# Four pairs ahead of the repeating step, rounded halves for the feed-forward's first products, and another order of the step

## The chip, the cores and the metric

The kernel runs on one core of one Trainium2 chip. The metric is device time in microseconds (us), the median of several runs; smaller is better. TensorE does the matrix products and transposes, VectorE and ScalarE read its results from PSUM (eight banks of 128 x 512 float32), GpSimd works on SBUF alone, and the DMA queues load and store.

## The reference

Sixteen batches of 128 tokens x 128 features pass a gated cross-attention over a context of 120 x 96, then two layers of windowed attention with a gated feed-forward, and a gated residual at the end. Cut to what matters here:

```python
def _layer(x, wqkv, qs, ksc, wo, lg, lb, w1, b1, w2, b2):
    h = shift_token(x)
    q, k, v = jnp.split(h @ wqkv, 3, axis=-1)     # 8 heads of 64
    q, k = rotary_xpos(l2norm(q) * qs, l2norm(k) * ksc)
    x = x + local_attention(q, k, v) @ wo
    h = shift_token(x)
    h = (h - mu) / jnp.sqrt(var + 1e-05) * lg + lb
    a, g = jnp.split(h @ w1 + b1, 2, axis=-1)     # 341 + 341 columns
    return x + (a * jax.nn.gelu(g, approximate=False)) @ w2 + b2
```

All inputs and the output are float32.

## The kernel before

**Work.** The cross-attention runs on pairs of batches (eight pairs). The layers run on 32 batch-layer items i (16 batches, then the same for layer 1). The feed-forward runs on groups of four items: seven full groups 0 to 6, and the last four items as two groups of two, 7 and 8. The residual stream is held transposed in `xs`, features on partitions.

**Step.** Every engine runs the same loop over a step number n and calls, in a written order, the functions whose item, pair or group is due: `project_k(n+5)`, `project_q(n+4)`, `squares` and `turns` (rotary products), `rows_q/rows_k(n+2)` (transposes), `scores_(n+2)`, `maxima_(n+1)` on VectorE, `weights(n+1)` (the exponentials, with `pp` and its sums) on ScalarE, `normalise(n+1)` on GpSimd, `weights_T(n+1)` (transposes of the probabilities), `weights_out` (their copy `pT` to SBUF, on ScalarE), `attend(n+1)`, `out_proj(n)`. On TensorE a step begins with `rows_k` and ends with scores, `weights_T`, `project_k` and `attend`. Each engine executes in its written order, so one waiting instruction holds all behind it. Lines such as `if s.n == -17` place single calls that have no fixed place in the loop: those of the first pairs and of the last two groups.

**Group in the step.** For group g, step 4g+4 holds `deviation`, `variance`, `dev_rstd` and `normed_h` (the normalised `hn`); step 4g+5, here called the gate step, holds three products `gate_in_0/1/2` of 128, 128 and 85 rows x 512 columns; step 4g+6, the value step, holds `value_in_0/1/2` and the three `gate` operations on VectorE; step 4g+7 the three products `back`. `gelu` on ScalarE (tile `gl`) stands in the gate step, between two table loads (Gelu's table and back to that of logarithm and exponential). `group_high` (VectorE, a cast to `h_hi`) and `group_low` (GpSimd, the rest `h_lo`) prepare layer 1's input.

**Two kinds of product.** The products of `project_*` use rounded halves: `h_hi`, `h_lo` and `wqkv_hi`, `wqkv_lo` are of type float32r, and three products (L505, L506, L507: high by high, high by low, low by high) are summed in PSUM. All others are float32 products; each shows two records in the trace. `hidden`, which all six first products of a feed-forward group call, is one float32 product (L730) of `w1g`, the weights times the norm's gain, and `hn`.

**First pairs.** Pairs from XP = 2 on run inside the repeating step; pairs 0 and 1 are placed by hand ahead of it. The loads of x and context come in three pieces: batches 0 to 1 on ScalarE's queue, 2 to 7 and 8 to 15 on SyncE's. Step -2 holds the scores of item 0.

## Time and profile before

| | us |
|---|---|
| median of 3 runs | 400.29 (395.24 to 403.95) |
| the profiled execution | 399.71 |
| its span in the trace | 397.9 |
| span by what runs: before the first scores at 48.27 | 48.3 |
| up to step 9's scores at 165.65 | 117.4 |
| from there to the last scores' end at 367.12 | 201.5 |
| tail | 30.8 |

The profiled execution took 1.8 us more than its span. Between 165.65 and 326.92, four steps take 40.3 us on average (161.27 us for 16 steps). Engine shares of the span are TensorE 90%, VectorE 84%, ScalarE 78%, GpSimd 59%.

### The profile page before, as it was taken

The page shows a single profiled execution, that of the slowest core. Times are in us where ns is not written, and L with a number is a line of the kernel's source. Part 1 is how long each engine was busy: PE and PEld are TensorE (multiplying, and loading weights), DVE is VectorE, ACT ScalarE, POOL GpSimd, SP SyncE. Part 2 cuts the span into 40 slices and gives each one's busy share as a digit, 9 for nine tenths or more (in the row PEclk, how much of TensorE's full clock was granted, in tenths as well). Part 3 has the DMA queues.
Part 4 walks back from the last instruction along what each step waited for, and adds up shares of the span by engine and source line. Part 5 has one row for each costly group of instructions (what it writes and reads, how often), then busy time and mean ns, then how long its engine had stood idle before and what let it go on. Part 6 is the DMA issues. An engine that isn't in the chain of part 4 may idle for free.

```text
span 397.9 us, 8200 instructions
## 1 busy us (share of the span) xinstructions
PE 359.7 (90%) x2502; PEld 263.1 (66%) x2502; DVE 336.0 (84%) x1286; ACT 308.4 (78%) x976; POOL 235.3 (59%) x260
## 2 busy tenths in 40 slices
PE   2888669899999999999999999999999999999895
PEld 1676548677776767667666677667666766666663
DVE  3697797999986999998899889998999889975535
ACT  3575658898989879986897689868986898678852
POOL 2197777797756659757564755575557554662200
PEclk9966888999999999999999999999999999999999
DMA  8900000000000000000000000000000000000001
GB/s 227 331 4 0 2 1 2 2 2 2 2 1 2 0 2 0 2 2 1 2 0 2 2 2 2 1 2 1 2 2 0 2 1 2 29 0 2 27 2 53
DMA packets 3472, 7.14 MB, mean 18 GB/s; under 512 B 403, under 2 KB 1973, under 8 KB 3429
## 3 DMA queue, kind: packets, MB, share of 16 engines
q1 hardware_dynamic: 3005, 6.13, 4.6%
q0 software_dynamic: 144, 0.26, 0.4%
q8 instruction: 21, 0.34, 0.4%
q10 hardware_dynamic: 279, 0.22, 0.2%
q14 instruction: 23, 0.18, 0.1%
HBM read 5.57 MB, written 1.05 MB: 17 GB/s over the span
## 4 chain that ended last, share of the span: by engine, by line
PE 64%; DVE 19%; ACT 7%; issue 6%; DMA 2%; POOL 1%; SPq 0%; DVEq 0%; POOLq 0%
PE ps L730 8%; PE ps L689 7%; PE ps L698 6%; PE ps L661 5%; PE ps L780 5%; PE ps L677 4%; PE ps L505 4%; PE ps L507 4%; PE ps L506 4%; DVE pp L1376 3%; PE ps L644 3%; DVE sn L1358 3%; PE ps L634 3%; DVE cs L1355 3%; ACT pT L1076 2%
## 5 line engine op out<-in xcount | busy, mean ns | idle before, releaser
L1071 ACT ACTIVATE pp<-pp,nm 128x128 f32<-128x128 f32 x256 | 99.1, 392 | 3.0 <-DVE nm L1376 2.8
L410 POOL TENSOR_TENSOR cs<-cs,sn 128x512 f32<-128x512 f32 x64 | 82.2, 1299 | 0.0
L403 POOL TENSOR_TENSOR pp<-pp,pri 128x512 f32<-128x512 f32 x64 | 66.7, 1042 | 16.5 <-DVE pri L1383 14.3
L1376 DVE CUSTOM_DVE_ANT_0 pp<-ps,msk,rr 128x128 f32<-128x128 f32 x256 | 74.3, 346 | 0.4
L423 POOL TENSOR_SCALAR ssc<-ss 128x16 f32<-128x16 f32 x32 | 7.9, 248 | 99.9 <-DVE ss L1365 99.9
L1076 ACT ACTIVATE pT<-ps 128x512 f32<-128x512 f32 x64 | 34.8, 596 | 36.2 <-PE ps L677 36.1
L1071 ACT ACTIVATION_READ_ACCUMULATOR pp<-pp,nm 128x1 f32 x256 | 49.0, 191 | 0.0
L730 PE MATMUL ps<-hn,w1g 128*128 128x512 f32 (+3 forms) x108 | 47.8, 555 | 1.2 <-DVE sn L1358 0.9
L505 PE MATMUL ps<-wqkv_hi,h_hi 128*128 128x512 f32 x96 | 45.9, 478 | 2.7 <-DVE sn L1358 2.4
L1358 DVE TENSOR_TENSOR sn<-ps,stab 128x256 f32<-128x256 f32 x128 | 47.6, 413 | 0.0
L661 PEld LDWEIGHTS ps<-kT,qT 64*128 64x128 f32 x512 | 31.9, 191 | 21.9 <-issue 15.8
L1355 DVE TENSOR_TENSOR cs<-ps,ctab 128x512 f32<-128x512 f32 x64 | 43.9, 686 | 2.9 <-ACT sqr L1059 1.4
L689 PE MATMUL ps<-pT,vv 128*64 128x128 f32 x512 | 35.0, 277 | 8.9 <-ACT pT L1076 8.6
L1365 DVE TENSOR_REDUCE ss<-sqr 128x8 f32<-128x512 f32 x64 | 42.5, 665 | 0.0
L689 PEld LDWEIGHTS ps<-pT,vv 128*64 128x64 f32 x512 | 28.2, 136 | 21.2 <-issue 21.2
L1059 ACT ACTIVATE sqr<-ps 128x512 f32<-128x512 f32 x64 | 37.6, 588 | 3.6 <-PE ps L507 2.7
L661 PE MATMUL ps<-kT,qT 64*128 64x128 f32 x512 | 38.1, 289 | 1.5 <-DVE kT L1387 1.4
L507 PE MATMUL ps<-wqkv_hi,h_lo 128*128 128x512 f32 x96 | 38.9, 405 | 0.0
L506 PE MATMUL ps<-wqkv_lo,h_hi 128*128 128x512 f32 x96 | 38.8, 405 | 0.0
L698 PEld LDWEIGHTS ps<-oT,wo_raw 128*128 128x128 f32 x256 | 32.5, 192 | 7.0 <-issue 6.2
L417 POOL TENSOR_TENSOR cs<-cs,rr 128x512 f32<-128x512 f32 x32 | 33.5, 1048 | 2.9 <-ACT rr L1065 2.7
L677 PE MATMUL ps<-idn,pp 128*128 128x128 f32 x256 | 35.0, 279 | 0.2 <-ACT gl L1102 0.2
(132 smaller groups left out, 750.5 us busy)
## 6 DMA issues: line engine op xcount, KB each, us to landing
wqkv_raw<-in_L_ffn_wqkv_dram SPq DMA_DIRECT2D x2, 768.0 KB, 12.8
out_dram<-xt SPq DMA_DIRECT2D x3, 256.0 KB, 2.4
w_raw<-in_w_dram SPq DMA_DIRECT2D x1, 682.0 KB, 13.0
xt<-in_x_dram SPq DMA_DIRECT2D x1, 512.0 KB, 9.2
wo_raw<-in_wo_dram SPq DMA_DIRECT2D x1, 512.0 KB
xt<-in_x_dram SPq DMA_DIRECT2D x1, 384.0 KB, 6.4
ct<-in_ctx_dram SPq DMA_DIRECT2D x1, 360.0 KB, 10.0
ct<-in_ctx_dram SPq DMA_DIRECT2D x1, 270.0 KB, 6.8
```

Source lines behind the costliest of these rows:

```text
L403: T(pp[m.j][:, a, :, :], pp[m.j][:, a, :, :], pri[m.j][:, a * 4:a * 4 + 4].unsqueeze(2).to_broadcast([128, PAIRS, 128]), ALU.mult).then_in ...
L410: T(cs[m.j][:, part], cs[m.j][:, part], sn[m.j][:, part], ALU.add).then_inc((aq_done, ak_done)[s], 1)
L505: mm(ps[:, part, :], hi, whi, start=True, stop=False)
L507: mm(ps[:, part, :], lo, whi, start=False, stop=True).then_inc((q_ps, k_ps, v_ps)[part], 1)
L661: last = mm(ps[:, SA + a, c * 128:(c + 1) * 128], qT[m.j][r, c, :], kT[m.j][r, c, :], start=True, stop=True)
L689: last = mm(ps[a * 64:a * 64 + 64, OB, c * 128:(c + 1) * 128], vv[m.j][:, h * DH:(h + 1) * DH], pT[m.j][:, a, c, :], start=True, stop=True)
L698: last = mm(ps[:, OB, Y], wo_raw[:, m.layer, c, :], oT[m.j][:, c, :], start=(c == 0), stop=(c == PAIRS - 1))
L730: mm(ps[0:m, bank, t.w], w1g[:, layer, s * HID + o:s * HID + o + m], hg, start=True, stop=True).then_inc((ha_ps, hg_ps)[s][c], 1)
L1071: A(pp[m.j][:, a, c, :], pp[m.j][:, a, c, :], ACT.Exp, bias=nm[m.j][:, a * 4 + c:a * 4 + c + 1], scale=-1.0, accum_out=psum_[m.j][:, a * 4 ...
L1355: V.tensor_tensor(heads(cs[m.j], s), x_, ctab[:, m.layer, s, :].unsqueeze(1).to_broadcast([128, HEADS, DH]), ALU.mult)
L1358: last = V.tensor_tensor(heads(sn[m.j], s)[:, :, o_], x_[:, :, i_], stab[:, m.layer, s, o_].unsqueeze(1).to_broadcast([128, HEADS, 32]), A ...
L1376: last = V.tensor_tensor_reduce(out=pp[m.j][:, a, c, :], in0=ps[:, SA + a, c * 128:(c + 1) * 128], in1=msk[:], scale=rr[m.j][:, h:h + 1], ...
```

## The change

- `hidden` becomes three products of float32r halves: `w1_hi` x `h_hi`, `w1_lo` x `h_hi`, `w1_hi` x `h_lo`. Here `h_hi` and `h_lo` are halves of the normalised `hn`, written over the group's former halves. ScalarE makes the high halves (`normed_high`, `gain_high`), GpSimd the low ones (`normed_low`, `gain_low`). `w1_in` now scales `w1_raw` in place.
- XP is 4: pairs 0 to 3 are placed by hand. The loads of batches 2 to 7 are two pieces, SyncE waits for the pieces of batches 0 and 1 before it issues them, and `wqkv` of layer 0 is loaded ahead of batches 8 to 15. GpSimd waits for the first context piece before its three table loads.
- All places in the step are written anew, with other PSUM banks and so other waits. `group_high` moves from group(-6) to group(-5), so to the same step as the next group's `normed_h`.
- ScalarE's table loads are placed by a helper that loads only when the function needs another table.

```diff
-XP = 2
+XP = 4
-        w1g = sb("w1g", [D, DEPTH, 2 * HID])
+        w1_hi, w1_lo = sb("w1_hi", [D, DEPTH, 2 * HID], F32R), sb("w1_lo", [D, DEPTH, 2 * HID], F32R)
-        HA_B, HG_B = ((SB, OB, VB), (QB, TQ, SB), (VB, QB, OB)), ((TQ, TK, OB), (VB, OB, TQ), (KB, OB, TQ))
+        HA_B, HG_B = ((KB, QB, QB), (TQ, TQ, TK), (TK, TK, TQ)), ((KB, OB, KB), (TK, TK, TQ), (TQ, VB, KB))
-        XCH = CCH = ((0, 2), (2, 8), (8, 16))
+        XCH = CCH = ((0, 2), (2, 4), (4, 8), (8, 16))
...
+            sp.wait_ge(ld_x[0], 16)
+            sp.wait_ge(ld_c[0], 16)
+            for k in range(1, 4):
+                if k == 3:
+                    sp.dma_start(wqkv_raw[:, 0, :], wqkv[0]).then_inc(ld_w[0], 16)
...
+            def gain_low(l):
+                pool.wait_ge(w1h_done[l], 1)
+                T(w1_lo[:, l, :], w1_raw[:, l, :], w1_hi[:, l, :].bitcast(F32), ALU.subtract).then_inc(w1l_done[l], 1)
+            def normed_low(g):
+                pool.wait_ge(nh_done, g + 1)
+                at = Group(g).at
+                T(h_lo[:, at, :], hn[:, at, :], h_hi[:, at, :].bitcast(F32), ALU.subtract).then_inc(nl_done, 1)
...
             def rows_q(m):
                 pe.wait_ge(aq_done, m.i + 1)
+                passed(u_ready[1], groups_by(m.i - 5))
...
             def hidden(g, c, s, banks):
-                pe.wait_ge(hn_ready, g + 1)
-                hg = hn[:, t.at, :].rearrange("p b n -> p (b n)")
-                mm(ps[0:m, bank, t.w], w1g[:, layer, s * HID + o:s * HID + o + m], hg, start=True, stop=True).then_inc(
-                    (ha_ps, hg_ps)[s][c], 1)
+                pe.wait_ge(nl_done, g + 1)
+                hi, lo = h_hi[:, t.at, :], h_lo[:, t.at, :]
+                at = slice(s * HID + o, s * HID + o + m)
+                mm(ps[0:m, bank, t.w], w1_hi[:, layer, at], hi, start=True, stop=False)
+                mm(ps[0:m, bank, t.w], w1_lo[:, layer, at], hi, start=False, stop=False)
+                mm(ps[0:m, bank, t.w], w1_hi[:, layer, at], lo, start=False, stop=True).then_inc((ha_ps, hg_ps)[s][c], 1)
...
+            def gain_high(l):
+                act.wait_ge(layer_w1[l], 1)
+                A(w1_hi[:, l, :], w1_raw[:, l, :], ACT.Copy).then_inc(w1h_done[l], 1)
+            def normed_high(g):
+                act.wait_ge(hn_ready, g + 1)
+                at = Group(g).at
+                A(h_hi[:, at, :], hn[:, at, :], ACT.Copy).then_inc(nh_done, 1)
...
# VectorE's step, the first pairs
-                if s.n == -43:
-                    stats(1)
-                if s.n == -43:
-                    tokens_normed(0)
+                if s.n == -40:
+                    tokens_normed(0)
+                if s.n == -37:
+                    stats(1)
+                    context_normed(0)
```

**First place: TensorE, value step of a full group.** Before, one value product stands behind `attend` (L689), one behind `project_q`, one behind `out_proj` (L698):

```order
L689 MATMUL ps<-pT0,vv0 64x128 x8
L730 MATMUL ps<-hn,w1g 128x512
L644 MATMUL ps<-idn,cs0 128x128 x4
...
L507 MATMUL ps<-wqkv_hi,h_lo 128x512
L730 MATMUL ps<-hn,w1g 128x512
L634 MATMUL ps<-idn,cs0 128x128 x4
L698 MATMUL ps<-oT0,wo_raw 128x128 x4
L730 MATMUL ps<-hn,w1g 85x512
L661 MATMUL ps<-kT0,qT0 128x128 x8
```

Now:

```order
L550 MATMUL ps<-wqkv_hi,h_lo 128x512
L766 MATMUL ps<-h_hi,w1_hi 128x512
L767 MATMUL ps<-h_hi,w1_lo 128x512
L768 MATMUL ps<-h_lo,w1_hi 128x512
...
L766 MATMUL ps<-h_hi,w1_hi 85x512
L767 MATMUL ps<-h_hi,w1_lo 85x512
L768 MATMUL ps<-h_lo,w1_hi 85x512
L670 MATMUL ps<-idn,cs0 128x128 x4
L733 MATMUL ps<-oT0,wo_raw 128x128 x4
L695 MATMUL ps<-kT0,qT0 128x128 x8
```

All nine value products now stand between `project_q` and `rows_q`, and nothing between `out_proj` and the scores.

**Second place: ScalarE, gate step of a full group.** Before:

```order
L1065 ACTIVATE rr0<-lns0,backt 128x16
L1059 ACTIVATE sqr1<-ps 128x512
L1199 ACT_TABLE_LOAD
L1102 ACTIVATE gl<-ps,b1_all 128x512
L1102 ACTIVATE gl<-ps,b1_all 85x512
L1076 ACTIVATE pT0<-ps 128x512 x2
L1102 ACTIVATE gl<-ps,b1_all 128x512
L1212 ACT_TABLE_LOAD
L1059 ACTIVATE sqr0<-ps 128x512
```

Now:

```order
L1183 ACTIVATE rr0<-lns0,backt 128x16
L1100 ACT_TABLE_LOAD
L1223 ACTIVATE gl<-ps,b1_all 85x512
L1176 ACTIVATE sqr1<-ps 128x512
L1223 ACTIVATE gl<-ps,b1_all 128x512 x2
L1195 ACTIVATE pT0<-ps 128x512 x2
L1176 ACTIVATE sqr0<-ps 128x512
L1100 ACT_TABLE_LOAD
```

The third Gelu has moved ahead of the copies of `pT`, for which `attend` waits. (In group 0's gate step the second table load and the two short operations of `norm_out` also stand ahead of them.)

**Third place: GpSimd, around the scores of item 0.** Before (L410 rotates, L423 is `clamped`, L355 the low half of the value weights, L417 `unit_k`):

```order
L410 TENSOR_TENSOR cs1<-cs1,sn1 128x512
L423 TENSOR_SCALAR ssc1<-ss1 128x16
L355 TENSOR_TENSOR wqkv_lo<-wqkv_raw,wqkv_hi 128x512
L417 TENSOR_TENSOR cs1<-cs1,rr1 128x512
L410 TENSOR_TENSOR cs1<-cs1,sn1 128x512
L375 TENSOR_SCALAR hn<-xt,mv,r1 128x128 x2
```

Now:

```order
L361 TENSOR_TENSOR wqkv_lo<-wqkv_raw,wqkv_hi 128x512
L427 TENSOR_TENSOR cs1<-cs1,sn1 128x512
L440 TENSOR_SCALAR ssc1<-ss1 128x16
L434 TENSOR_TENSOR cs1<-cs1,rr1 128x512
L427 TENSOR_TENSOR cs1<-cs1,sn1 128x512
```

The weights' low half has moved from behind `clamped` to ahead of the rotation of k, so `unit_k`, which waits for ScalarE's `lengths`, now follows `clamped` directly.

## Rows read from the trace of the kernel before

**Rows 1.** The page: busy time by engine, and the granted clock in 40 slices.
```profile
PE 359.7 (90%) x2502; PEld 263.1 (66%) x2502; DVE 336.0 (84%) x1286; ACT 308.4 (78%) x976; POOL 235.3 (59%) x260
PEclk9966888999999999999999999999999999999999
```
**Rows 2.** Busy time by stretch (length, PE, PEld, DVE, ACT, POOL, granted clock, DMA share).
```profile
165.65:367.12 201.47, 194.63 (x1420) 137.97 (x1420) 179.41 (x664) 163.22 (x517) 119.18 (x122) 1.00 0.01 3
```
**Rows 3.** The chain that ended last, group 5's gate and value steps: start, us, what.
```profile
284.40 2.57 PE ps L730 x6
...
289.79 0.24 issue
290.03 1.09 PE ps L689 x16
291.12 1.06 PE ps L730 x2
...
293.58 0.24 PE ps L506
...
294.05 0.86 PE ps L730 x2
...
296.24 1.05 PE ps L730 x2
```
**Rows 4.** TensorE's groups with shapes apart: busy, mean ns of one.
```profile
L506 PE MATMUL ps<-wqkv_lo,h_hi 128*128 128x512 f32 x96 | 38.8, 405 | 0.0
...
L730 PE MATMUL ps<-hn,w1g 128*128 128x512 f32 x56 | 28.2, 605 | 0.9 <-DVE sn L1358 0.9
```
**Rows 5.** ScalarE's timeline in the same gate step.
```profile
284.93 0.31 ACT L1065 ACTIVATE rr<-lns,backt 128x16 f32<-128x16 f32 x1
...
285.74 1.28 ACT L1199 ACT_TABLE_LOAD   x1
287.03 1.26 ACT L1102 ACTIVATE gl<-ps,b_all 128x512 f32<-128x512 f32 x2
288.69 1.09 ACT L1076 ACTIVATE pT<-ps 128x512 f32<-128x512 f32 x2 [0.40 <-PE ps L677]
```
**Rows 6.** VectorE's timeline: a wait for `rstd`, and three casts to `h_hi`.
```profile
26.26 0.26 DVE L1322 CAST h_hi<-xs 128x256 fp32r<-128x256 f32 x1
...
48.52 3.60 DVE L1322 CAST h_hi<-xs 128x256 fp32r<-128x256 f32 x1
...
278.31 0.69 DVE L1403 TENSOR_TENSOR hn<-ps,rstd 128x512 f32<-128x512 f32 x1 [1.45 <-ACT rstd L1096]
...
286.77 1.28 DVE L1328 CAST h_hi<-xs 128x512 fp32r<-128x512 f32 x1
```
**Rows 7.** GpSimd's timeline beside the second of them.
```profile
48.43 1.27 POOL L355 TENSOR_TENSOR wqkv_lo<-wqkv_raw,wqkv_hi 128x512 fp32r<-128x512 f32 x1
49.66 1.04 POOL L417 TENSOR_TENSOR cs<-cs,rr 128x512 f32<-128x512 f32 x1
50.67 1.29 POOL L410 TENSOR_TENSOR cs<-cs,sn 128x512 f32<-128x512 f32 x1
```
**Rows 8.** The chain that ended last, from that cast on.
```profile
49.52 2.53 issue
```
**Rows 9.** VectorE's timeline at the start.
```profile
9.03 0.29 DVE L1252 BATCH_NORM_STATS2 bst<-xt 128x6 f32<-128x128 f32 x1 [2.87 <-DMA ct<-in_ctx_dram]
...
10.17 0.57 DVE L1277 TENSOR_SCALAR hn<-xt,mv,r 128x128 f32<-128x128 f32 x2
```
**Rows 10.** Groups with shapes apart, ScalarE and GpSimd: copies and differences like the added ones.
```profile
L1006 ACT ACTIVATE wqkv_hi<-wqkv_raw 128x512 fp32r<-128x512 f32 x6 | 3.4, 616 | 0.0
L1089 ACT ACTIVATE dsq<-ps 128x256 f32<-128x256 f32 x2 | 0.8, 376 | 0.0
...
L392 POOL TENSOR_TENSOR h_lo<-xs,h_hi 128x256 fp32r<-128x256 f32 x8 | 5.4, 681 | 1.4 <-DVE h_hi L1322 1.4
L398 POOL TENSOR_TENSOR h_lo<-xs,h_hi 128x512 fp32r<-128x512 f32 x4 | 4.7, 1185 | 0.0
```

More of the change, by code:

```diff
@@ L1099, in gelu @@
                 o, m = CH[c]
+                table("gelu_and_others")
                 act.wait_ge(hg_ps[c], g + 1)
@@ new lines, in step @@
+                if s.n == 6:
+                    w1_in(1)
+                if s.on(1):
+                    maxima_(s.at(1), 1)
+                if s.n == -3:
+                    maxima(2)
+                if s.n == 39:
+                    gate(7, 1)
+                if s.n == -6:
+                    token_high(1)
+                if s.n == -2:
+                    w1_in(0)
+                if s.n == 34:
+                    gate(7, 0)
+                if s.pair(8) is not None:
+                    maxima(s.pair(8))
@@ new lines, in step @@
+                if s.n == 46:
+                    update(8)
+                if s.pair(8) is not None:
+                    context_sums(s.pair(8))
+                if s.n == -13:
+                    residual(1)
+                if s.on(1):
+                    inverse(s.at(1), 1)
+                if s.n == 45:
+                    gate(8, 2)
+                if s.on(4):
+                    squared(s.at(4), 1)
+                if s.group(-5) is not None and s.group(-5) < NG:
+                    group_high(s.group(-5))
@@ new lines, in step @@
+                if s.pair(7) is not None:
+                    token_high(s.pair(7))
+                if s.n == -17:
+                    residual(0)
+                if s.pair(8) is not None:
+                    residual(s.pair(8))
+                if s.n == -15:
+                    stack_in(0)
+                if s.n == -19:
+                    maxima(0)
+                if s.group(-3) is not None:
+                    gate(s.group(-3), 2)
+                if s.n == -1:
+                    residual(3)
```

906 lines of the change are left out of this document (504 added, 402 removed).

## Prediction

> **What bounds the kernel now.** I read the page first: TensorE is busy 90% of the span, VectorE 84%, ScalarE 78%, GpSimd 59%, and the granted clock is below 0.9 in five of 40 slices only, the third to the seventh, 20 to 70 us [rows 1]. Then the stretches: between step 9's scores (165.65) and the last (367.12) TensorE is busy 194.63 of 201.47 us at a granted clock of 1.00, VectorE 179.41, ScalarE 163.22 and GpSimd 119.18 [rows 2]. TensorE's row of work sets the pace there, and 6.8 us of idle time in 201 is all that a better order alone could take out. Then the chain of waits through one gate and one value step [rows 3]: it stays on TensorE, with one short stop, 0.24 us ahead of `attend` (290.03), which waits for the copy of the probabilities. Last I read the groups and timelines for the price of each kind of instruction. The ends of the kernel are of another sort: before the first scores (48.3 us) and in the tail (30.8 us) chains between engines set the time, and there an order does count.
>
> **The changed product.** The column of busy time misleads here. By groups [rows 4] a float32 product shows two records of 605 ns, 1.21 us, and a float32r product 405, so three of them would take 1.22 and gain nothing. But matmuls are pipelined; what the row of work pays is the pitch from one to the next. The chain [rows 3] has the gate step's three float32 products (six records) in 2.57 us, 0.86 each, and the single products of the value step at 1.06, 0.86 and 1.05. It has a float32r product at 0.24. A triple is then 3 x 0.24 = 0.72. A gate step's three: 2.57 - 2.16 = 0.41 less. A value step's three: 2.97 - 2.16 = 0.81 less, since the 0.2 us that two of the single products pay beside transposes and attention products is paid once at most when all nine stand together. For a full group 1.2 us, for seven groups 8.5 us if all of it lies on the path.
>
> It doesn't all do so. In the gate step `attend` already waits for ScalarE [rows 3]. ScalarE's row there [rows 5]: `rr` ends at 285.24, the table load starts at 285.74 (it stands behind one square), two Gelus 0.6 apart, then at 288.69 two copies `pT`, 1.09 us, and only then the third Gelu. Afterwards the load starts at 285.24, and three Gelus, the square and the two copies follow: 285.24 + 1.28 + 3 x 0.57 (a Gelu's share beside the square's 0.5, from 1.26 for two) + 0.5 + 1.1 = 289.85, against 289.78 before. So the copies come no earlier, TensorE arrives 0.4 us earlier, and waits: the gate step's 0.4 goes into a longer stop ahead of `attend`, and what remains is the value step's 0.8, less a little for the new waits in `rows_q`. I take 0.7 a group, 7 x 0.7 = 4.9 us. The ends: all of it kept and the bubble gone, 1.24 x 7 = 8.7; and 0.2 x 7 = 1.4 if the copy into `h_hi` (0.6, before a step's first square) and `rows_q`'s wait for VectorE's gate come on top.
>
> The Trainium skill, "FP8 and Floating Point Precision", TensorE Precision Notes, has it that true FP32 is four passes through the array, H*H, H*L, L*H and L*L. Three passes would by that be three quarters of 0.86, 0.645 where the trace's pitch gives 0.72; the group's gain would be 1.03 from the 14 full products and more, and seven groups would give some 9 us by that estimate in place of 8.5, before what the wait swallows.
>
> **The work added.** For each full group ScalarE copies `hn` to `h_hi`, about 0.6 us by the nearest copy, and GpSimd forms `h_lo`, 1.19 [rows 10]; for the two small groups 0.38 and 0.68. Both stand in the step with `normed_h`. There `hn` starts at 278.31 and takes 0.69 [rows 6]; so 279.00 + 1.1 of `pT` copies + 0.6 + 1.2 puts the last half at 281.9, and the gate products of the next step start at 284.40 [rows 3]: 2.5 us of cover. ScalarE has 38 us of room in the stretch [rows 2] and pays 7 x 0.6 = 4.3; GpSimd has 82 and pays 8.3. I cost both at nothing; if the cover went, 0.6 + 1.2 a group would come in. The two weight halves (682 columns, about 0.8 and 1.6 us by width) are made once per layer, well ahead. The cast `group_high` moves to the same step as `normed_h`, one step later, where VectorE waits 1.45 us for `rstd` [rows 6]; the cast of 1.28 fits in that wait, so VectorE gives back up to 1.3 us in four steps. VectorE isn't the bound, and I count nothing for it.
>
> **Group 0's gate step.** The second table load now stands ahead of the `pT` copies there, with the two operations of `norm_out`. One load is 1.28 us and what follows starts with no gap [rows 5]; `attend` waits for it in full, as it already waited before: +1.3, from 0 (if the first pairs' work has run ahead) to 2. The same skill, "ScalarE: Activation LUTs", What ACT_TABLE_LOAD costs, gives a load some 1.38 us of drain besides, 2.66 together. The row speaks against it: the Gelu's record begins at 287.03 and the load's ends at 287.02. With the drain step 5 would cost 2.7 in place of 1.3, a shift of 1.4 us that leaves the forecast within its range.
>
> **The start.** VectorE's `stats(1)` waited 2.87 us for the second context piece, until 9.03, and the first pair's `hn` stood behind it at 10.17 [rows 9]. Now that `hn` stands behind `folded`, which waits for TensorE, and `stats(1)` behind it. The first pair leaves about a microsecond earlier; against this the pieces of batches 2 to 7 are issued only after the first have landed, and the layer's weights after those. I take -1, from -2 to +2.
>
> **The stall at 48.5.** One cast to `h_hi` takes 3.60 us; the same cast at 26.26 takes 0.26 [rows 6]. In the chain 2.53 us stand behind it as issue [rows 8]. GpSimd's rows say why: three operations lie end to end, 48.43 to 51.96 [rows 7], and the cast ends at 52.12, just behind the last. So this cast to float32r waits while GpSimd is busy, and gets its turn only in a gap. Now `wqkv_lo` stands ahead of the rotation, and `unit_k`, which waits for ScalarE's `lengths`, follows `clamped`: there is a gap of GpSimd behind `clamped`. I take -2.5, what the chain shows; the ends are -4, if TensorE, which idles behind it, also gets its full clock earlier (0.8 in the slices around it [rows 1]), and +3.5, if the stall only moves, to `w1_in(0)`, which now stands between `turns` at that step, or to `token_high(2)`.
>
> **The tail.** Groups 7 and 8 get a copy of 0.38 and a difference of 0.68 in line [rows 10] between `hn` and the first products, which for group 8 nothing hides. The float32r products save some of it, and `deviation(8)` no longer stands behind four float32 products. +0.5, from 0 to 1.5.
>
> **Sum.** -4.9 + 1.3 - 1 - 2.5 + 0.5 = -6.6 us on the profiled 399.7, so 393.1. That execution lies 0.6 below the median of the runs shown, 400.3, which spread over 8.7; I state 393.0. A measurement of this kernel tells about 2%, 8 us, from no change; 392.3 is the line.
>
> **The rivals.**
> (A) The forecast, 389 to 397, about 393: chance 0.48.
> (B) Only the groups gain. The stall moves, and the later loads eat what the start wins: 399.7 - 4.9 + 1.3 + 0.5 = 396.6, some 397. For it: the chain runs through several engines there, and one freed wait has the next close behind. Against it: the 2.53 us stand in the chain as they are. Chance 0.22.
> (E) All of it comes through. Gate and value steps keep 1.0 a group or more (7.0), the start -2, the stall -4, step 5 and tail nearly nothing: 399.7 - 13 = 386.7, about 386. For it: the load moves up 0.5 us in the gate step, and if ScalarE runs further ahead because VectorE has its cast hidden, the bubble closes. Chance 0.17.
> (C) Three products are no cheaper. If the pitch behind different weights is not 0.24 but the busy 405 ns of the groups [rows 4], a triple takes 1.22 against 0.86 to 1.06, +0.2 to +0.36 x 42, up to +10; that the chain's 0.24 comes from the same three kinds of product speaks against it. With the column's other reading (1.29 against 1.21) +3.4 and a time of about 400. Chance 0.06.
> (D) Slower. The cast's stall [rows 6, 7] isn't rare but becomes a part of the step: `group_high` in the step of `normed_h` now meets GpSimd's rotations and `h_lo`, back to back. Each such stall is 3.60 - 0.26 = 3.3 us on VectorE, which has only 22 us of room in the stretch [rows 2] and hands `turns` and `maxima` on to TensorE. Seven of them cost 23 us, of which the 1.45 us of wait and half of the rest may be hidden: 7 x (3.3 - 1.45) = 13, less the forecast's 6.6: 399.7 + 6.4 = 406, and 408 with one in the first pairs. The change is slower than before from four such stalls on (6.6 / 1.85), and by over 2% from eight. Against it: the cast at 286.77, in the middle of the repeating step, takes 1.28 us for 512 columns, more than twice 0.26 but far from a stall [rows 6]. Chance 0.07.
>
> **How the numbers follow.** The likeliest is A, 393.0. Range: 386 takes in most of E, 400 all of B and C; outside remain half of E, D and a corner of B, some 0.18. Faster by over 2% (below 392.3): E's 0.17, half of A (0.23) and 0.02 of B: 0.42. Slower by over 2% (above 408.3): most of D, where the stalls are more than seven, and the upper end of C, with the unknown places of a wholly new order, 0.07. Within: 0.51.
>
> **What would show it.** In the changed kernel's profile: a triple of products at 0.70 to 0.78 us from its first to the next work (right), or above 0.86 (C). The period of four steps between scores about 39.5 us where it was 40.3. TensorE's stop ahead of `attend` in a gate step about 0.6 us where 0.24 stood, and in group 0's gate step about 1.5. `h_lo` of a group done 2 us or more ahead of the gate products. The first scores at about 45, and no cast of 256 columns above 1 us between 40 and 55. In the tail one `h_lo` in the chain, 0.7 us. The forecast is wrong if VectorE's `hn` or `rstd` come late because the casts stall (`hidden` would then wait for `nl_done`), if the first scores are later than 48.3, or if TensorE's granted clock falls between the first pairs, where four pairs now run ahead by hand and a longer wait would leave it idle.

## The result, and the profile of the changed kernel

| us | before | changed |
|---|---|---|
| median of 20 runs | 399.25 (394.67 to 405.30) | 394.50 (392.32 to 399.78) |
| ratio, 95% interval | | 0.9937 (0.9908 to 0.9967) |
| the profiled execution, its span | 399.71, 397.9 | 396.63, 394.8 |

The change is worth 0.6%, clear of noise and under 2%. The medians lie 4.75 us apart, the ratio makes it 2.5 us: the ratio leaves out executions of either kernel far above its shortest, and the kernel before has more of those. Forecast was 393.0 from 399.7, 1.7%.

The page: TensorE is as busy as before, GpSimd busier, VectorE less [rows 1].

```profile
PE 357.0 (90%) x2556; PEld 271.7 (69%) x2556; DVE 330.0 (84%) x1286; ACT 312.6 (79%) x987; POOL 249.4 (63%) x271
PEclk9999888999999899999999999999999999999999
```

There is a new dip of the granted clock in the 14th slice, which [rows 1] lack. Where the time went is read from the starts of the scores (the first row of L661 or L695 in each step) in the two timelines; the starts are the profile's, the rest are differences:

| stretch | before | changed | difference |
|---|---|---|---|
| to the scores of step 4 | 110.34 | 108.49 | -1.85 |
| steps 5 and 6 | 23.47 | 26.49 | +3.02 |
| steps 7 to 13 | 71.95 | 71.19 | -0.76 |
| step 14 | 11.26 | 10.31 | -0.95 |
| steps 15 to 29 | 148.94 | 147.57 | -1.37 |
| from there to the end | 31.94 | 30.75 | -1.19 |

Group 4's four steps, 20 to 23, take 9.57, 10.08, 10.32 and 10.05 before, 9.57, 9.59, 10.33 and 10.21 after: 40.02 and 39.70. (An interval n runs from the scores of step n-1 to those of step n. Group 4's gate products end interval 21, its value products interval 22.)

The chain that ended last, through the same stretch as [rows 3]:

```profile
277.87 0.98 ACT pT L1195 x2
278.85 0.52 ACT h_hi L1120
...
284.36 1.28 ACT L1100
...
286.82 0.58 ACT gl L1223
287.41 0.14 issue
287.54 0.63 PE ps L712 x4
...
289.00 0.20 issue
289.20 1.09 PE ps L724 x16
...
292.27 0.24 PE ps L766
292.51 0.23 PE ps L767
292.74 0.23 PE ps L768
...
293.68 0.44 PE ps L766
```

TensorE's timeline has the wait in that chain:

```profile
287.54 0.63 PE L712 MATMUL ps<-idn,pp 128*128 128x128 f32 x4 [0.27 <-ACT gl L1223]
```

Two things are to be seen. A triple is 0.71 or 0.70 from its first to the next work, as forecast; the third of a value step is 0.90, since its first record takes 0.44 of the row, and all nine products run from 292.27 to 294.58, 2.31. And the chain has left TensorE: it runs through ScalarE from the copies `pT` at 277.87, over the new copy into `h_hi` (L1120), to the Gelu at 286.82, for which TensorE's transposes `weights_T` (L712) wait, and after them `attend` (L724). From scores to `attend` it is 285.52 to 289.20, 3.68 us, against 286.90 to 290.03, 3.13, before; from `attend` to the next scores 6.65 against 7.19. The added 0.55 stands at the transposes: the eight took 0.85 of TensorE's row before (287.99 to 288.84) and take 1.42 now (286.61 to 288.03), because the second four wait for a Gelu.

Steps 5 and 6, in TensorE's timeline and in the busy time by stretch (columns as in [rows 2]):

```profile
126.76 1.52 PE L724 MATMUL ps<-pT,vv 128*64 128x128 f32 x16 [1.98 <-ACT pT L1195]
...
129.98 0.63 PE L549 MATMUL ps<-wqkv_lo,h_hi 128*128 128x512 f32 x1
...
131.00 0.39 PE L549 MATMUL ps<-wqkv_lo,h_hi 128*128 128x512 f32 x1
```
```profile
121.73:134.98 13.25, 11.27 (x78) 9.20 (x77) 9.19 (x33) 10.37 (x33) 5.92 (x7) 0.87 0.00 1
```

`attend` stops for 1.98 us behind the second table load, and the same 128x512 product that takes 0.39 takes 0.63 at 129.98. The granted clock is 0.87 over the interval; it is 1.00 up to 126.73 and 0.50 to 0.52 from 127.73 to 130.73, so it fell from 2.4 to 1.2 GHz behind the stop.

### The profile page after: what moved, and what is told of

It reads as the page before. It is cut to its first block, busy times and chain, and to the rows that moved or that the text cites. A ratio compares the mean times of both kernels' runs of the same rounds, so it can differ in the third digit from the quotient of the medians.

```text
span 394.8 us, 8336 instructions
## 1 busy us (share of the span) xinstructions
PE 357.0 (90%) x2556; PEld 271.7 (69%) x2556; DVE 330.0 (84%) x1286; ACT 312.6 (79%) x987; POOL 249.4 (63%) x271
## 4 chain that ended last, share of the span: by engine, by line
PE 52%; ACT 25%; DVE 13%; issue 5%; DMA 3%; POOL 3%; SPq 0%; ACTq 0%; DVEq 0%; POOLq 0%
PE ps L724 6%; PE ps L820 5%; ACT pp L1190 5%; PE ps L733 5%; PE ps L712 4%; PE ps L695 4%; PE ps L548 3%; PE ps L549 3%; PE ps L550 3%; PE ps L679 3%; ACT pT L1195 3%; DMA ct<-in_ctx_dram 3%; ACT L1100 3%; ACT gl L1223 3%; DVE pp L1539 3%
## 5 line engine op out<-in xcount | busy, mean ns | idle before, releaser
L724 PE MATMUL ps<-pT,vv 128*64 128x128 f32 x512 | 35.5, 279 | 10.4 <-ACT pT L1195 10.2
L724 PEld LDWEIGHTS ps<-pT,vv 128*64 128x64 f32 x512 | 28.4, 137 | 22.6 <-issue 22.6
L695 PEld LDWEIGHTS ps<-kT,qT 64*128 64x128 f32 x512 | 31.9, 191 | 14.8 <-issue 8.7
L695 PE MATMUL ps<-kT,qT 64*128 64x128 f32 x512 | 38.1, 289 | 1.1 <-DVE kT L1550 0.8
L712 PE MATMUL ps<-idn,pp 128*128 128x128 f32 x256 | 36.9, 285 | 1.3 <-ACT gl L1223 1.3
L733 PE MATMUL ps<-oT,wo_raw 128*128 128x128 f32 x256 | 33.8, 275 | 0.0
## 6 DMA issues: line engine op xcount, KB each, us to landing
w_raw<-in_w_dram SPq DMA_DIRECT2D x1, 682.0 KB, 11.7
```

The lines of the kernel that those rows point to most:

```text
L695: last = mm(ps[:, SA + a, c * 128:(c + 1) * 128], qT[m.j][r, c, :], kT[m.j][r, c, :], start=True, stop=True)
L712: last = tr(ps[:, TQ + a, c * 128:(c + 1) * 128], pp[m.j][:, a, c, :], idn[:])
L724: last = mm(ps[a * 64:a * 64 + 64, OB, c * 128:(c + 1) * 128], vv[m.j][:, h * DH:(h + 1) * DH], pT[m.j][:, a, c, :], start=True, stop=True)
L733: last = mm(ps[:, OB, Y], wo_raw[:, m.layer, c, :], oT[m.j][:, c, :], start=(c == 0), stop=(c == PAIRS - 1))
```

## The experiments

All run against the kernel before on the same chip, 12 executions each; "period" is steps 20 to 23 in the profiled execution, 40.02 before and 39.70 changed.

| label | median | ratio (interval) | period |
|---|---|---|---|
| f32_products | 396.81 | 0.9978 (0.9929 to 1.0027) | 39.91 |
| value_f32 | 395.38 | 0.9936 (0.9899 to 0.9974) | 39.81 |
| before_triples | 397.27 | 0.9955 (0.9911 to 0.9998) | 39.69 |
| copy_twice | 398.19 | 1.0004 (0.9963 to 1.0045) | 40.19 |
| h_hi_on_gpsimd | 394.57 | 0.9918 (0.9871 to 0.9965) | 39.70 |
| gelu_behind | 401.52 | 1.0089 (1.0045 to 1.0133) | 40.91 |
| norm_late | 395.78 | 0.9957 (0.9920 to 0.9994) | 39.69 |
| norm_early | 394.46 | 0.9915 (0.9877 to 0.9953) | 39.68 |
| w1_at_13 | 394.55 | 0.9942 (0.9901 to 0.9983) | 39.69 |
| before_low_early | 397.01 | 0.9947 (0.9905 to 0.9989) | 40.04 |
| after_low_late | 395.46 | 0.9934 (0.9887 to 0.9980) | 39.68 |
| before_max | 399.24 | 1.0006 (0.9955 to 1.0056) | 40.02 |
| after_max | 394.88 | 0.9925 (0.9885 to 0.9965) | 39.69 |
| sp_no_wait | 394.21 | 0.9926 (0.9884 to 0.9968) | 39.68 |
| start_context_late | 395.34 | 0.9952 (0.9910 to 0.9993) | 39.70 |
| spread_wait | 395.62 | 0.9950 (0.9912 to 0.9989) | 39.70 |
| old_order_both | 395.05 | 0.9930 (0.9894 to 0.9965) | 39.69 |
| old_order_spread | 393.37 | 0.9916 (0.9881 to 0.9950) | 39.68 |

The intervals are about 1% wide, so most of these kernels can't be told apart by time. The period repeats to 0.02 us between kernels that agree in those steps, and the verdicts on single steps rest on it; each is read from one profiled execution of its kernel.

### What the products are worth

**f32_products**

```diff
-mm(ps[0:m, bank, t.w], w1_hi[...], hi, ...)   # and two more
+mm(ps[0:m, bank, t.w], w1_raw[:, layer, at], hg, start=True, stop=True)
```

> The changed kernel with the six first products of each group as one float32 product each (w1 times gain by hn), all copies and halves still made and waited for. By pitch (0.23 a float32r product against 0.86 for a float32 one, 0.16 a product) a value step gets 0.5 us longer; a gate step stays as it is if ScalarE sets its end, and gets 0.5 longer if TensorE does. Theory: +0.5 to 0.7 us a group, +4 to +5 us in all with the tail. Rival: by the column of busy time (three at 0.40 against two at 0.60) no change, 0 to +0.5 us in all. Other rival: both steps pay in full, +7 us.

Measured: gate interval 10.09, value interval 10.20, the next 10.06; 39.91. The tail takes 31.57 us (span 394.4 less 362.83) where the changed kernel's takes 30.75. The gate products' 0.5 is on the path, the value products' is not: the theory is right on the gate step; the value step, for which it asked 0.5, got 0.13 shorter. The next step gets 0.15 shorter as well, so of the gate step's 0.50 only 0.2 a group remains in the period, and +0.8 in the tail.

**value_f32**

```diff
+if s == 0 and g < GT:
+    mm(ps[0:m, bank, t.w], w1_raw[:, layer, at], hg, start=True, stop=True); return
```

> The changed kernel with only the value products of the full groups as single float32 products; the gate products stay triples. Theory: a value step's end is set by ScalarE, so these products have room there: the intervals between scores stay at 9.60 (gate step), 10.2 to 10.3 (value step), 10.2 (next step), 0 us in all. Rival, by my forecast: the value step gets 0.5 us longer or more, +3.5 us in all.

Measured: 9.69, 10.50, 10.06: gate and value interval together are 20.19 in place of 19.92 (how these two share it differs by 0.1 from one execution to the next), the next is 0.15 shorter. Nine float32r products in place of three float32 ones are worth 0.1 us a group, not 0.8; the rival falls, and the theory's nought is short by that 0.1.

**before_triples** (the kernel before, with the diff's `hidden`, copies and differences for groups 0 to 6)

```diff
+if s.group(-1) is not None: normed_high(s.group(-1))   # ScalarE, end of the step
+if s.group(-2) is not None: normed_low(s.group(-2))    # GpSimd, behind rotate q
```

> The kernel before, with the products of the full groups 0 to 6 as triples of halves (ScalarE and GpSimd make the halves at the places of the changed kernel; groups 7 and 8 stay float32). Theory: the gate step's three products are on TensorE's path in both orders, so its interval falls from 10.08 by 0.4 to 0.5, the value step's does not fall, and ScalarE's copy may cost up to 0.5 where its row has no gap: four steps 39.7 to 40.1 against 40.15, -0.5 to -3 us in all. Rival: the gain needs the new order, and the four steps stay at 40.15 or above. By my forecast, where each triple saves 0.14 to 0.34: -0.7 or more a group, 39.4.

Measured: 9.70, 10.23 and 10.19 for steps 21 to 23, period 39.69. The old order with the new products has the whole gain of the repeating step; the new order adds nothing to it. (Outside the period, step 14 takes 10.31 in the new order and 11.44 here.)

### Who sets the gate and value steps

**copy_twice**

```diff
+if g < GT: A(lnl[...], hn[:, at, :], ACT.Copy)
 A(h_hi[:, at, :], hn[:, at, :], ACT.Copy)
```

> The changed kernel, in which ScalarE copies the normalised hn of each full group twice (first into the scratch lnl, then into h_hi). My forecast costed one such copy at nothing, since GpSimd's half is done well ahead of the gate products: then a second copy costs 0 to 0.5 us in all. Theory after the result: ScalarE's row from the step with normed_h to pT of the gate step has no gap, so every copy there is paid in full: +0.5 us for each of seven groups, +3.5 us in all, seen as a longer stop of TensorE ahead of weights_T or attend.

Measured: the gate interval is 10.08 in place of 9.59 to 9.70, the other three of the period are as they were. What I costed at nothing costs 0.49 a group of the period once it is done twice. (This execution also has a 128x512 cast of 3.79 us in step 8, and step 9 takes 13.61. Its step 5 is shorter than the changed kernel's, 12.49 for 13.24; see `after_low_late`.)

**h_hi_on_gpsimd**

```diff
-normed_high(s.group(-1))            # ScalarE
+nc.gpsimd.tensor_copy(h_hi[:, at, :], hn[:, at, :])
```

> The changed kernel, with the copy of hn into h_hi of the full groups made by GpSimd ahead of its h_lo, in place of ScalarE. A second copy on ScalarE cost 0.47 us in each gate step's interval. Theory A: ScalarE alone sets that interval, and without the copy it falls by 0.5 a group, -3 us in all. Theory B: ScalarE and TensorE are level there (float32 products added 0.5 to the same interval as well), and it falls by 0 to 0.1 a group: 0 to -1 us in all, ScalarE merely getting room. Third: GpSimd's longer row delays the rotations: +0.2 a group or more.

Measured: 9.67, 10.25, 10.21, period 39.70: theory B. ScalarE, freed of the copy, has to wait for TensorE's product instead, and its row from there to the Gelus is again without a gap:

```profile
276.97 0.60 ACT L1181 ACTIVATE sqr<-ps 128x512 f32<-128x512 f32 x1 [0.33 <-PE ps L555]
```

The first copy is free and the second isn't: ScalarE and TensorE arrive together, and each holds if the other is relieved.

**gelu_behind** (`gate_in_0` of groups 1 to 6 into the bank of v, its Gelu behind `pT`)

> The changed kernel, with gate_in_0's product of groups 1 to 6 in the bank of v and its Gelu behind the copies pT, as the third Gelu stood before the change. Theory: the Gelu ahead of pT swallows what the gate products win; behind them attend comes 0.5 us earlier in six gate steps, whose interval between scores falls from 10.2 to 9.7: -3 us in all. Rival: ScalarE is late as a whole, so that what attend wins the next step's squares and weights lose: 0 to -1 us in all.

Measured: the gate interval is 11.10 (+1.5), the value interval 10.05 (-0.28). In the chain 1.18 us stand ahead of the gate products, at 287.06, that the changed kernel's doesn't have:

```profile
286.17 0.89 PE ps L737 x8
287.06 1.18 issue
288.24 0.47 PE ps L770
```

By what I changed, the new bank is free only once VectorE has copied v, which is late in the step; so the product waits where it did not. The profile names no engine for this wait. The 0.28 won behind it may be the part that the Gelu ahead of `pT` swallows, but the later scores can also have given ScalarE time, so that part isn't shown. The Gelu's old place without that bank wasn't tried.

### The table load of step 5

**norm_late**

```diff
-if s.pair(8) is not None: norm_out(s.pair(8))
+if s.pair(8) is not None and s.n != 5: norm_out(s.pair(8))
 weights_out(s.at(1), 0); weights_out(s.at(1), 1)
+if s.n == 5: norm_out(s.pair(8))
```

> The changed kernel, with norm_out (and so the second table load) of step 5 behind the copies pT. Theory: that load ahead of pT made attend wait 1.98 us, and the idle TensorE then ran some 2 us of work at the lower clock, so steps 5 and 6 (26.5 us between scores against 23.5 before) get back 2.5 to 3 us: the stop ahead of attend falls to 0.2 to 0.7 us, granted clock 1.00 in step 6, total about 3 us less than the changed kernel. Rival: the added time in step 6 belongs to w1_in(1) and the casts of layer 1's weights, which moved there; then only the 1.3 us of the load come back and step 6 stays above 12 us.

Measured: `attend` no longer waits for it, and step 6 takes 13.68 at a granted clock of 0.88. TensorE's timeline shows why:

```profile
123.91 1.09 PE L724 MATMUL ps<-pT,vv 128*64 128x128 f32 x16
127.24 0.44 PE L658 MATMUL ps<-idn,zo 128*128 128x128 f32 x2 [2.24 <-POOL zo L402]
```

The stop of 1.98 has become one of 2.24 a little later, at `out_T`, which waits for GpSimd's `zo` and so for `norm_out` behind the load. The theory falls. The rival does too, by `w1_at_13` below: its step 6 takes 13.44 without `w1_in(1)`.

**norm_early** (`norm_out` of step 5 ahead of the first Gelu)

> The changed kernel, with norm_out of step 5 ahead of the first Gelu and so of the first table load, as it stood before the change (with the load behind pT the wait only moved: TensorE waited 2.24 us for zo, which waits for norm_out). Theory: neither attend nor zo is late then, the step between scores 5 and 6 falls from 11.9 (13.3 to 13.7 in executions in which the clock fell) to 10.5 to 10.9, that is -1.2 to -2.8 us in all. Rival: the Gelus, held up until the residual's statistics are there (about 1.5 us), make weights_T wait for their banks, and the step stays at 11.5 or more.

Measured: step 5 13.22, step 6 12.54 at a granted clock of 1.00; the rival is right. The stop moved a third time, into three pieces:

```profile
122.13 0.63 PE L712 MATMUL ps<-idn,pp 128*128 128x128 f32 x4 [0.61 <-ACT gl L1223]
123.46 0.63 PE L712 MATMUL ps<-idn,pp 128*128 128x128 f32 x4 [0.70 <-ACT gl L1223]
...
129.30 0.50 PE L766 MATMUL ps<-h_hi,w_hi 128*128 128x512 f32 x1 [0.88 <-ACT xs L1170]
```

0.61 + 0.70 + 0.88 = 2.19. Wherever `norm_out` stands, TensorE loses 2.0 to 2.2 us there, to two loads of 1.28, three Gelus and the last pairs' work on ScalarE. What differs is the clock. With the changed kernel's order and products step 6 took 11.89 to 11.91 at a granted clock of 1.00 in five executions (`sp_no_wait` is one) and 13.24 to 13.44 in four, 0.87 in the changed kernel's own:

```profile
120.37:132.27 11.90, 9.91 (x77) 7.72 (x77) 8.94 (x33) 10.26 (x33) 5.78 (x7) 1.00 0.01 1
```

So the stop costs 1.2 us against the 10.70 of before, and 1.35 more in the executions in which the clock falls behind it. With the stop in pieces the clock stayed up in both profiled executions (this one and `spread_wait`), and step 6 takes 12.54, 0.64 more than in one piece with the clock up. `norm_early` spread from 392.86 to 395.86 in 12 executions, the changed kernel from 392.32 to 399.78 in 20; that the pieces are the reason wasn't isolated.

**w1_at_13**

```diff
-if s.n == 6: w1_in(1)
+if s.n == 13: w1_in(1)        # and gain_high(1) in step 14
```

> The changed kernel with w1_in(1) back in step 13, and its high half in step 14. My forecast took that move for neutral. Theory after the result: step 14 was 11.26 us before and is 10.31 now because this operation (1.58 us beside a busy GpSimd) left it, while at step 6 VectorE waits for TensorE anyway and it is free: moved back it costs +0.9 us, in step 14, and step 6 stays at 13.2. Rival: step 6 falls by 0.5 us or more and the sum is nought.

Measured: step 14 takes 10.33, step 6 13.44 (the clock down). Both theories fall: the operation takes 1.37 us there and costs nothing. Before, two operations stood end to end on VectorE in the chain:

```profile
205.53 1.28 DVE L1328 CAST h_hi<-xs 128x512 fp32r<-128x512 f32 x1
206.73 1.58 DVE L1340 TENSOR_SCALAR w1g<-w_raw,first 128x682 f32<-128x682 f32 x1
```

With `group_high` gone from that step the other has room: that is how I read the 0.95 us that step 14 gained. `group_high` alone was not moved back, so the reading is argued, not shown.

### The stall beside GpSimd

**before_low_early**

```diff
-if s.n == -1: weights_low(0, 2)      # ahead of unit_k
+if s.n == -2: weights_low(0, 2)      # ahead of rotate k
```

> The kernel before with one line moved: GpSimd makes the low half of the value weights in step -2 ahead of k's rotation, in place of step -1 ahead of unit_k, as in the changed kernel. Theory: the 128x256 cast at 48.5 us no longer lies behind three GpSimd operations end to end; it takes 0.3 to 0.8 us in place of 3.60, and the scores of item 1 (61.07) come 2 to 3 us earlier; by step 9 about 2 us remain. Rival: the stall moves to the next operation of its kind and less than 1 us remains.

Measured: the cast takes 1.10 us, step -1 10.36 us (12.80 before), step 4's scores come at 103.83. But in step 8 of the same execution a cast of the same kind stalls, beside a row of GpSimd without a gap:

```profile
148.49 4.04 DVE L1322 CAST h_hi<-xs 128x256 fp32r<-128x256 f32 x1
```
```profile
148.11 2.04 POOL L403 TENSOR_TENSOR pp<-pp,pri 128x512 f32<-128x512 f32 x2
150.11 1.05 POOL L417 TENSOR_TENSOR cs<-cs,rr 128x512 f32<-128x512 f32 x1
151.11 1.27 POOL L410 TENSOR_TENSOR cs<-cs,sn 128x512 f32<-128x512 f32 x1
```

It ends at 152.53, GpSimd's row at 152.38, and step 9 takes 14.12 us for 10.10. The theory is right on step -1; but step 9's scores come at 163.18 for 165.65, and the first scores alone were 3.80 earlier here (44.47), so by step 9 nothing is left of it, as the rival has it.

**after_low_late** (the changed kernel with that line back)

> The changed kernel with the low half of the value weights back in step -1, ahead of unit_k. Theory: a cast of VectorE near 47 us stalls again by about 3 us and steps -1 to 0 end about 2 us later. Rival: in the new order no operation of VectorE meets those three of GpSimd, the change is below 0.5 us, and the gain at the first scores has another cause.

Measured: no cast over 1.3 us, step -1 10.47. The rival is right: the new order meets no stall there, whatever that line's place.

It meets a shorter one of the same kind later. `nmb`, an operation on two columns that takes 0.17 us in step 3 before, starts in the changed kernel beside a rotation of GpSimd and ends with it (94.12 and 94.09):

```profile
92.96 1.16 DVE L1460 TENSOR_SCALAR nmb<-nmx 128x2 f32<-128x2 f32 x1
```
```profile
92.78 1.31 POOL L427 TENSOR_TENSOR cs<-cs,sn 128x512 f32<-128x512 f32 x1
```

It takes 1.13 to 1.16 in all fourteen profiles of the new order, whose step 3 takes 10.81 to 10.96 against 9.85 to 9.99 in the six of the old: about 1 us of the start. In step 5 the same operation takes 1.11 (114.27) where it took 0.17 before; there the old order with triples has it too (1.12 in `before_triples`), so it comes with GpSimd's added work. `copy_twice` escapes it (0.36), and its step 5 is 0.75 shorter.

**before_max** and **after_max**

```diff
-V.tensor_copy(h_hi[:, at, :], xs[:, at, 0:N])
+V.tensor_tensor(h_hi[:, at, :], xs[:, at, 0:N], xs[:, at, 0:N], ALU.max)
```

> The kernel before, with VectorE's casts to h_hi (token_high and group_high) written as the maximum of xs with itself, an operation with two inputs and the same result. Theory: only the cast form waits behind GpSimd (3.60 us at 48.5 in the profile of before, 4.04 at 148.5 in another run, 3.79 at 153.1 in a third), where it does so differs from run to run, and TensorE's clock falls behind it; so without that form no operation to h_hi takes over 1.1 us, the 9 us between the shortest and longest execution shrink, and the median is 2 to 4 us lower. Rival: GpSimd's load holds up VectorE whatever the form: the two-input operation stalls as well, and the median stays.

> The changed kernel, with the same two casts written as a maximum of xs with itself. Theory: casts of 0.8 to 1.3 us in four steps become 0.35 to 0.5, and the occasional stall of 3.8 us at step 8 or 9 is gone: the median falls by 0 to 2 us and is less spread (by less than in the kernel before, which would show that the changed order meets fewer stalls). Rival: the two-input form is slower for 512 columns or stalls too: no change.

Measured:

```profile
44.94 3.71 DVE L1322 TENSOR_TENSOR h_hi<-xs 128x256 fp32r<-128x256 f32 x1
```

The two-input form stalls as the cast does; the form is not the cause, and neither median moves. The stalled operations (`h_hi`, `nmb`, `w1g`) all read and write SBUF alone, and copies of the same size from PSUM are not among them.

### The start, and versions put together

**sp_no_wait**

```diff
-sp.wait_ge(ld_x[0], 16)
-sp.wait_ge(ld_c[0], 16)
```

> The changed kernel without SyncE's two waits ahead of its loads, so the pieces of batches 2 to 7 are issued at once. In the changed kernel the context of batches 2 and 3 lands at 13.1 us (before: 2 to 7 at 8.9). Theory of the forecast: the waits are worth a little, the first pieces land earlier by them: without them the first scores (47.1) come 0 to 2 us later. Rival: the chain at the start runs through that second context piece, and without the waits the first scores come 1 to 3 us earlier.

Measured: the first scores come at 47.12, to the digit as with the waits. (The granted clock differed: 0.71, 0.50 and 0.77 from 20 to 35 in steps of 5 us here, 1.00 in the changed kernel.) No effect of the waits on the start is seen; that lies at the end of what the forecast's theory allowed.

**start_context_late** (`context_normed(3)` from step -6 to step -3, behind the rotation)

> The changed kernel, with GpSimd's context_normed of pair 3 behind the rotation of the first k in place of ahead of it. Theory: in the chain 1.34 us of that work (and more for pair 2) stand between the first h_lo and the rotation, so the first scores come 1.0 to 1.5 us earlier, at about 46, unless TensorE, whose context_T of pair 3 then waits, loses it again. Rival: what bounds the first scores is TensorE's own work for four pairs: 47.2 as before, or later by that wait.

Pair 4's counts now come ahead of pair 3's, so that pair 3's context is transposed before it is normalised: this kernel leaves out TensorE's wait for it, and its output is not the right one; its time alone is read. Measured: first scores at 48.26, 1.1 later. This piece alone is not the cause.

**spread_wait** (`norm_early`, `h_hi_on_gpsimd` and `sp_no_wait` together)

> The changed kernel with norm_out of step 5 ahead of the first table load, h_hi of the full groups on GpSimd, and no waits of SyncE. Theory: each is worth 0 to 0.3% and they do not touch each other; the steady period stays at 39.7, the stop of TensorE in steps 5 and 6 is spread over three places and its clock stays at 1.00 there, so the executions lie close together (standard deviation about 1 us where the changed kernel has 2): median 393.5 to 394.5, ratio to before 0.989 to 0.991. Rival: ScalarE freed of the copy has its weights ready earlier and the value step falls below 10.2: below 393.

Measured: 395.62, period 39.70, step 6 12.54. A 128x512 cast of 3.79 us at 154.54 makes step 9 13.51 in the profiled execution. The three are not seen to add up.

**old_order_both** (`before_triples` with `before_low_early`) and **old_order_spread** (with layer 1's three low halves in steps 8, 9 and 10 as well)

> The kernel before with two changes: triples of halves for groups 0 to 6, and the low half of the value weights in step -2 ahead of k's rotation. Theory: step -1's interval is 10.4 as in before_low_early (12.5 in before_triples), the scores of step 4 come at 104 to 106, from there on it goes as before_triples did (286.5 us to the end): span 390.5 to 392.5 where no stall falls into step 8 or 9, +3.9 where one does; median 393.5 to 395.5, at or below the changed kernel. Rival: the stall turns up at another place each time and the median stays at 397, as in before_triples.

> The same, with GpSimd's three low halves of layer 1's weights in steps 8, 9 and 10 in place of all in step 8. Theory: without 3.8 us of GpSimd work end to end ahead of step 8's rotation no cast meets a GpSimd row of over 3 us, the stall of 3.8 to 4.0 us at step 8 or 9 does not occur in any execution: the longest executions are 2 to 4 us shorter than in old_order_both and the median 0 to 2 lower. Rival: the row of normalise, unit_k and rotation (4.3 us) alone is what a cast waits behind, and the two kernels are alike.

Measured: 395.05 and 393.37, with step 4's scores at 105.11 and 106.96. Step -1 is 9.6 in both, and the next cast stalls for it: 3.23 us at 64.03 and at 65.88, step 1 12.12 where `before_triples` has 10.54. No stall at step 8 or 9 was seen in either profile, so what the spreading does for it stays open, though the longest execution is 396.07 (396.73 with the halves together; 399.78 for the changed kernel). `old_order_spread` has the lowest median of all, though its interval overlaps the changed kernel's: the old order with the new products and a few GpSimd operations placed otherwise does about as much as the whole rewritten order (0.9930 and 0.9916 against 0.9937).

## Why the prediction was wrong

It named the right direction and the right parts, and was too large by a factor of nearly three by the ratio (1.7% against 0.6%); by the medians 6.6 us were forecast and 4.75 came. That 394.50 lies near 393.0 is partly luck: terms missed in both directions. By its terms:

| term | forecast | measured, and by what |
|---|---|---|
| seven full groups | -4.9, 0.7 each | -0.32 a group (periods), -2.1 in steps 7 to 13 and 15 to 29 |
| group 0's steps 5 and 6: table load | +1.3 (+0.6 with group 0's 0.7, which is in the line above) | +1.65 with the clock up (+1.20 in step 6 by the stop, +0.45 in step 5, where `nmb` waits), +3.0 in the profile |
| start and cast stall | -3.5 | -1.85 in the profiled pair, no gain against other profiles of the old order, see below |
| tail | +0.5 | -1.19, of which -0.8 the products |
| VectorE's moves (`group_high`, `w1_in(1)`) | 0 | -0.95 in step 14 |

**The groups** are the step that failed. The pitches were right, the triples take 0.70, and the gate interval fell by 0.49. What failed is "what remains is the value step's 0.8". Two things are in it. First, 2.97 less 2.16 counted as the product's own the 0.2 that is paid where one kind of work follows another: the nine products take 2.31, the transposes behind `attend` now 0.59 for 0.44, and from `attend` to the scores the gain is 0.54. Second, I let the Gelu's place swallow the gate step's gain at `attend`, which it did not touch (that interval fell in full), but the wait it makes stands in the value interval and ate 0.55 there, ahead of the second four transposes `weights_T`. The step behind is 0.16 longer (10.21 for 10.05; its first product `back` takes 1.01 of the row for 0.86). So a group gains 0.49, then 0.54 less 0.55, and loses 0.16: 0.32. `value_f32` confirms it: without the value triples the period is 0.11 longer, where my step wants 0.8. The stop ahead of `attend` was forecast at 0.6; it is 0.20, and what I looked for there stands at L712. A sum over one engine's row missed that its waits merely change place.

**The copy into `h_hi`** was costed at nothing with 2.5 us of cover for GpSimd's half. The cover is there (the half is done at 280.71, I had said 281.9), but the copy has another follower: ScalarE's own row runs without a gap from it to the Gelu. It happens to be level with TensorE (`copy_twice` +0.49, `h_hi_on_gpsimd` 0), so the term was right by luck. GpSimd's half was costed at nothing too, and in step 5 that was wrong: `nmb` waits there behind the longer row of GpSimd, and `copy_twice`, which escapes this wait, is 0.75 shorter in that step.

**Group 0's table load** was right in mechanism and place: `attend` waits 1.98, and step 6 is 1.20 longer with the clock up, for which 1.3 was forecast. I missed that the clock falls behind such a stop, which adds 1.35 us in some executions, and that moving the load doesn't remove the stop: three places gave 1.98, 2.24 and 2.19. The old order with the new products has no such stop: `before_triples` takes 13.27 and 10.88, 1.0 less than the changed kernel with its clock up.

**The stall at 48.5** was read rightly as a wait behind GpSimd, and it recurs: 3.60, 3.71 and 3.58 us in three executions of the old order, with step -1 at 12.80, 12.57 and 12.50; the changed kernel's takes 10.78. That it was the move of `wqkv_lo` that would cure it holds for the old order alone, and there the stall turns up elsewhere. But "gets its turn only in a gap" does not fit GpSimd's own timeline, in which a fourth operation follows [rows 7] with no gap, while the cast ends at 52.12:

```profile
51.93 1.64 POOL L375 TENSOR_SCALAR hn<-xt,mv,r 128x128 f32<-128x128 f32 x2
```

So the cast got in behind the last of three `TENSOR_TENSOR` operations, which take two tensors, and beside a `TENSOR_SCALAR`, which takes one and a value per partition. Five of the eight stalls end so, the other three at the end of GpSimd's row.

**The start** was measured against one execution. The scores of step -2 come at 46.75 to 47.44 in the changed kernel and all its variants but `start_context_late`. In the old order they came at 48.27 in the profile of before, and at 44.47, 44.68, 45.18, 45.63 and 47.49 in five variants, whose kernels differ little up to 30 us. The rows by stretch (before, then `before_max`) show the difference:

```profile
30.00:35.00 5.00, 5.00 (x19) 4.19 (x18) 2.82 (x6) 3.13 (x10) 4.13 (x7) 0.50 0.00 0
```
```profile
30.00:35.00 5.00, 4.02 (x22) 2.78 (x21) 4.62 (x11) 3.81 (x12) 4.41 (x7) 1.00 0.00 0
```

At a granted clock of 0.50 TensorE is busy all through and the chain waits for it; at 1.00 it isn't. `old_order_spread` (47.49) has 0.50 in that stretch as well, the three others 0.98 to 1.00. The new order doesn't depend on it so: `w1_at_13` has 0.50 to 0.60 from 20 to 35 and its first scores at 46.75. So the new order's start is some 2.5 us slower than the old one's best and a little over 1 faster than its worst, and far steadier. Its first normalised tokens are at 7.76 in place of 10.17, a gain of 2.4 that is gone by the first scores. The chain that ended last points at GpSimd, which normalises tokens and contexts of the added pairs where before TensorE's work stood:

```profile
31.19 2.20 POOL ct L382 x4
...
33.86 1.58 POOL hn L392 x2
35.44 1.34 POOL ct L382 x2
```

Only the last of the three was moved, without gain, so this stays a suspicion; SyncE's waits are not it. By step 4's scores the changed kernel and its variants stand at 106.11 to 109.72, the old order at 110.34 in the profile of before but at 103.83 to 106.96 in its five variants: the -1.85 of the profiled pair is no property of the order. Without it the terms are -0.76, +1.65, -0.95, -1.37 and -1.19, together -2.6, close to the ratio's 2.5.

**The tail** I had as slower for the added copy; the triples for group 6's value step and groups 7 and 8 win 0.8 there by `f32_products`, more than the copy costs. The `h_lo` that I expected in the chain of the tail isn't in it.

Of the rivals none took place as written: B's "the stall moves" happened in the new order only as `nmb`'s 1 us in step 3, C's equal cost is refuted by the gate interval, and D's stall was seen once each in two of the new order's fourteen profiled executions (both 3.79 us, in step 8), where D wanted four. The low end of the group term, "0.2 a group", for which I gave two reasons, was nearer than its middle.

**Slips in the working.** A triple of 0.645 in place of 0.72 would be 6 x 0.075 = 0.45 more a group and 11.7 us in seven, not some 9; the measured 0.70 and 0.71 lie between. C's upper end, 0.36 x 42, is 15 and not 10, so the range to 400 doesn't hold all of C. And `group_high` moved one step earlier, not later: it starts at 275.37 where it started at 286.77, and takes 0.91 for 1.28.

## What to carry to other kernels

A sum over one engine's row does not say what a cheaper operation is worth when another engine arrives at the same time. Follow the wait from interval to interval: before counting it as gone, look where it will stand next. A short operation that looks free, like the copy here, is free only up to the other engine's room. A stop that can't be removed may be better spread in pieces: in one piece step 6 took 11.90 or, where the clock fell, 13.24, and in pieces 12.54. And a start or a stall read from one execution needs a second one before it is entered in a sum: here the start alone differed by 3.8 us between executions of the same order.

## What the runs showed of the hardware

- A VectorE operation from SBUF to SBUF can wait behind several GpSimd operations in a row: 3.23 to 4.04 us for 0.26 to 0.9 us of work, eight times in these profiles, whether it has one tensor input or two. Each of the eight ends 0.15 to 0.29 us behind the end of a `TENSOR_TENSOR` of GpSimd; in five of them a `TENSOR_SCALAR` followed there without a gap. Other executions let the same operation in sooner (0.78 to 1.3 us). An operation on two columns waits as well, for one GpSimd operation (1.16 for 0.17).
- Behind a stop of TensorE of 2.0 to 2.2 us, the granted clock fell in some executions (step 6 at 13.24 to 13.68 us, five of them) and not in others (11.90). Where it fell, a product of 0.39 took 0.63, and the granted clock was 0.50 to 0.52 from 127.73 to 130.73.
- Between 20 and 35 us the granted clock differs between executions of the same work: 1.00 in the changed kernel, 0.50 to 0.60 in `w1_at_13`, which is alike up to there.
- A table load takes 1.28 us in all profiles, and where nothing else held up the next operation, it started 0.01 to 0.02 us behind it.
